# Hyperbolic attention stage: q, k and v kept unscaled beside their factors, with the multiplication moved to each head's preparation

## The reference, cut to what matters

```
q, k, v = heads(x @ Wq.T), heads(x @ Wk.T), heads(x @ Wv.T)       # x is layer-normalized
exp0(u) = tanh(sqrt(c)*|u|) * u / (sqrt(c)*|u|)                   # for q, k, v
dist = arccosh(max(1 + 2c*|q-k|^2 / ((1-c|q|^2)(1-c|k|^2)), 1+1e-5)) / sqrt(c)
weights = softmax(-beta*dist)                                     # 2048 x 2048 for each of 32 heads
out = weights @ log0(v)                                           # then exp0, log0, @ Wo.T, + x
```

## Time and profile before

| | us |
|---|---|
| median of 3 runs | 5894.83 (5894.81 to 5903.06) |
| the profiled execution | 5902.13 |
| its span in the profile | 5900.3 |
| ScalarE busy in the span | 4513.9 (77%) |
| VectorE busy | 4660.2 (79%) |
| TensorE matmul busy | 4364.9 (74%) |
| GpSimd busy | 1432.0 (24%) |

### The profile page before, as it was taken

How to read it: one execution, slowest core, us unless ns; L and a number is a source line. 1 busy time by engine, 2 the same in 40 slices (tenths; PEclk the granted TensorE clock), 3 DMA queues, 4 the chain that set the end, 5 groups by cost and what they waited for, 6 DMA issues and landing times. The chain is left out here.

```text
span 5900.3 us, 69208 instructions
## 1 busy us (share of the span) xinstructions
PE 4364.9 (74%) x22020; PEld 1837.5 (31%) x22020; DVE 4660.2 (79%) x7142; ACT 4513.9 (77%) x3668; POOL 1432.0 (24%) x1259
## 2 busy tenths in 40 slices
PE   8999999999999999546655665665565655655657
PEld 4555555555555556311111011111010111110105
DVE  7666666766666666589989899999998999998966
ACT  4555555555555554339999999999999999999993
POOL 0000000000000000234444444444444444444420
PEclk9999999999999998766666666666666667666667
DMA  1000000000000000169898989898989898989891
GB/s 39 5 5 5 5 7 7 5 5 6 5 5 5 5 2 1 34 171 192 182 193 182 193 182 193 182 193 182 193 182 194 182 193 182 194 182 194 180 197 62
DMA packets 149381, 637.99 MB, mean 108 GB/s; under 512 B 32662, under 2 KB 74840, under 8 KB 79064
## 3 DMA queue, kind: packets, MB, share of 16 engines
q0 software_dynamic: 73728, 536.90, 45.5%
q1 hardware_dynamic: 75224, 95.82, 4.8%
HBM read 69.46 MB, written 26.35 MB: 16 GB/s over the span
## 5 line engine op out<-in xcount | busy, mean ns | idle before, releaser
L1715 PE MATMUL psum<-b_qT,b_kT 126*128 126x512 bf16 x2048 | 921.8, 552 | 1116.0 <-DVE b_tiles L1445 1109.8
L1445 DVE SCALAR_TENSOR_TENSOR b_tiles<-b_ra_rep,b_cap,psum 128x1024 f32<-128x1024 f32 x1024 | 1263.0, 1274 | 281.9 <-DMA b_tiles<-b_tiles 182.1
L668 DVE CUSTOM_DVE_ANT_0 a_srow<-psum,a_bias 128x512 f32<-128x512 f32 (+3 forms) x1280 | 725.6, 607 | 494.2 <-PE psum L849 491.1
L727 ACT ACTIVATE a_pT<-psum 128x512 f32<-128x512 f32 (+3 forms) x1056 | 511.9, 527 | 657.2 <-PE psum L861 656.9
L1715 PEld LDWEIGHTS psum<-b_qT,b_kT 126*128 126x128 bf16 x2048 | 136.4, 108 | 2054.2 <-DVE b_tiles L1445 1882.7
L1452 DVE TENSOR_SCALAR b_tiles<-b_tiles 128x2048 f32<-128x2048 f32 x512 | 682.5, 1333 | 4.3
L861 PE MATMUL psum<-ident,a_srow 128*128 128x128 f32 x4352 | 625.6, 280 | 70.5 <-DVE a_pT L541 32.9
L1728 PE MATMUL psum<-b_tiles,b_v_aug 128*32 128x512 f32 x2736 | 592.0, 957 | 99.7 <-ACT b_tiles L1626 99.7
L1626 ACT ACTIVATE b_tiles<-b_tiles,b_sc 128x4096 f32<-128x4096 f32 x171 | 650.1, 3802 | 5.7
L1618 ACT ACTIVATE b_tiles<-b_tiles 128x4096 f32<-128x4096 f32 x171 | 613.3, 3610 | 35.4 <-DVE b_tiles L1088 34.5
L1295 POOL DMA_DIRECT2D b_tiles<-b_tiles x342 | 355.0, 1229 | 1172.9 <-ACT b_tiles L1618 1169.9
(11 more groups left out here) (215 smaller groups left out, 5338.8 us busy)
## 6 DMA issues: line engine op xcount, KB each, us to landing
b_tiles<-b_tiles POOLq DMA_DIRECT2D x342, 1024.0 KB, 12.9
X<-b_tiles POOLq DMA_DIRECT2D x170, 1024.0 KB, 13.2
b_ra_rep<-ra_scratch SPq DMA_DIRECT2D x32, 1024.0 KB, 13.8
row_scratch<-b_tiles SPq DMA_DIRECT2D x6, 2048.0 KB, 13.9
b_qk_raw<-row_scratch SPq DMA_DIRECT2D x31, 288.0 KB, 8.8
X<-in_x_dram SPq DMA_DIRECT2D x8, 512.0 KB, 6.6
a_wqk<-in_wqk_dram SPq DMA_DIRECT2D x32, 128.0 KB, 2.6
x_scratch<-X SPq DMA_DIRECT2D x4, 1024.0 KB, 10.6
```

The source lines that it names most:

```text
L668: nc.vector.tensor_tensor_reduce(out=srow[:, n % ROWS, h, a:z], in0=bank(c % 2 * 2 + h, 0, z - a), in1=bias[:, h, off + a:off + z], scale= ...
L1445: nc.vector.scalar_tensor_tensor(out=a[:, s * HALF:(s + 1) * HALF], in0=ra_rep[:, j, s * HALF:(s + 1) * HALF], scalar=cap[:, j, k:k + 1], ...
L1715: last = nc.tensor.matmul(half_ps(s)[:, i * BANK:(i + 1) * BANK], kT[:, j, k * P:(k + 1) * P], qT[:, j, cs], start=True, stop=True)
```

## The change: what it does

- `scale` is gone. `tok[b]` is stored to `row_scratch` as projected, and three rows more are stored beside it (F_Q, F_K, F_V: `arr` has seven rows for four). GpSimd's `prepare` and `take_v` multiply by the factor where they copied. Batch 0's q, k, v are stored as soon as its 16 tiles are copied, batch 1's (v first) as soon as all are, each ahead of the factors in SyncE's order.
- `factors` is in three parts. For batch 0, `lengths` is at n = 23 and the parts at n = 24, 26 and 28, each behind the normalization; ScalarE's roots are ahead of the tiles of group 5, the tanh behind them, and the transposes of `ra` one group later.
- Root batches: four of two chunks, then 126 of four; the weights that follow a batch's roots go up to the batch's first chunk.
- GpSimd squares every chunk with c % 4 == 2 from the first on; `first_use` waits are finer and stand with the engine that writes the slot.
- X is saved to its scratch only when the projection's weights are loaded.

```diff
-ROOTS, KEPT = 4, 4
+ROOTS = [2] * 4 + [4] * ((CHUNKS - 8) // 4)
...
-            return SQUARES[c % len(SQUARES)] if c >= NO_POOL else "D"
+            return SQUARES[c % len(SQUARES)]
...
-                step(engine.tensor_copy(aug[:, 0, :, 0:DB], rows(0)))
+                step(engine.tensor_tensor(aug[:, 0, :, 0:DB], rows(0), each(F_Q), ALU.mult))
...
-                step(engine.tensor_copy(aug[:, 1, :, 0:DB], rows(1)))
+                step(engine.tensor_tensor(aug[:, 1, :, 0:DB], rows(1), each(F_K), ALU.mult))
...
-            engine.tensor_copy(v_aug[:, g % 2, :, 0:DB], v).then_inc(S["v_ready"], 1)
+            engine.tensor_tensor(v_aug[:, g % 2, :, 0:DB], v, f.unsqueeze(2).to_broadcast([P, TB, DB]), ALU.mult
+                                 ).then_inc(S["v_ready"], 1)
...
+        def first_use(eng, slot):
+            if slot < 6:
+                eng.wait_ge(S["row_saved0"], 64)
+                eng.wait_ge(S["v_ready"], 1)
+            elif 6 <= slot < 10:
+                eng.wait_ge(S["row_saved1"], 48)
+            elif slot < 12:
+                eng.wait_ge(S["v_saved1"], 16)
...
+            sp.wait_ge(S["w_loaded"], 16)
...
+            sp.wait_ge(S["tok_copied"], TB)
+            for i in range(3):
+                store_row(0, i, S["row_saved0"])
+            store_factors(0)
+            sp.wait_ge(S["ra_stored"], 16)
+            load_ra(0)
+            sp.wait_ge(S["row_saved0"], 64)
+            load_qk(1)
+            load_v(1)
+            load_ra(1)
+            sp.wait_ge(S["tok_copied"], NT)
+            store_row(1, 2, S["v_saved1"])
+            for i in range(2):
+                store_row(1, i, S["row_saved1"])
+            store_factors(1)
...
-            def scale(b):
-                pool.wait_ge(S["factors_done"], b + 1)
-                pool.wait_ge(S["tok_copied"], (b + 1) * TB)
-                for i in SCALED[b]:
-                    dst = tok[b][:, i, :, :, :].rearrange("p h t d -> p (h t) d")
-                    f = tmp[:, FACTOR_OF[i], :].unsqueeze(2).to_broadcast([P, NF, DB])
-                    nc.gpsimd.tensor_tensor(dst, dst, f, ALU.mult).then_inc(S["tok_scaled"], 1)
-
-            scale(0)
-            pool.wait_ge(S["tok_scaled"], 3)
+            pool.wait_ge(S["factors_done"], 1)
+            pool.wait_ge(S["tok_copied"], TB)
...
-            scale(1)
...
+                if c < Y_BACK and by(c) == "P":
+                    first_use(pool, Y_SLOTS[c])
...
-                if n == TB + 4:
-                    factors(0)
+                if n == TB + 7:
+                    lengths(0)
+                if n >= TB + 8 and n % 2 == 0 and n < TB + 14:
+                    factors(0, (n - TB - 8) // 2)
...
-                if n == TB + 3:
-                    lengths(0)
...
+                if q == TB // 4 + 1:
+                    roots_all(0)
...
-                if q == TB // 4:
-                    roots_all(0)
+                if q == TB // 4 + 1:
                     tanhs(0)
-                if q == TB // 4 + 2:
+                if q == TB // 4 + 3:
                     ra_copy(0)
...
-                upto = z - KEPT if z < CHUNKS else CHUNKS
+                upto = a if z < CHUNKS else CHUNKS
```

More of the change, by code:

```diff
@@ L998, in stage_attn_b @@
         sc = sb("sc", [P, 24])
-        NS_Q, E_K, EN_K, CAP_K = range(4)
+        NS_Q, E_K, EN_K, CAP_K, F_Q, F_K, F_V = range(7)
         NF = TB * HB
@@ L1088, in square_by @@
             engine.tensor_tensor(y_slot(c), a, a, ALU.mult).then_inc(S["sq_" + name], 1)
-        root_batches = [(c, min(c + ROOTS, CHUNKS)) for c in range(0, CHUNKS, ROOTS)]
+        root_batches = [(sum(ROOTS[:n]), sum(ROOTS[:n + 1])) for n in range(len(ROOTS))]
+        assert root_batches[-1][1] == CHUNKS
         PREP = 17
@@ L1107, in of, with each @@
                 return f.unsqueeze(2)
+            def each(i):
+                return of(i).to_broadcast([P, TB, DB])
             def rows(i):
@@ L1212, in store_o, with store_row, store_factors @@
                 sp.dma_start(o_scratch[:, g * ROW_K:(g + 1) * ROW_K], o_raw[:, :]).then_inc(S["o_stored"], 16)
-            for b in range(BATCH):
+            def store_row(b, i, saved):
+                hs = slice(b * HB, (b + 1) * HB)
+                at = (0, ROW_K, ROW - ROW_K)[i]
+                sp.dma_start(rows[:, hs, at:at + ROW_K], tok[b][:, i, :, :, :].rearrange("p h t d -> p h (t d)")
+                             ).then_inc(saved, 16)
+            def store_factors(b):
                 hs = slice(b * HB, (b + 1) * HB)
@@ L1219, in _ @@
                 sp.wait_ge(S["factors_done"], b + 1)
[L1220 to L1234, removed]
+                sp.dma_start(rows[:, hs, ROW_F:ROW - ROW_K], arr[b].rearrange("p i h t -> p h i t")
+                             ).then_inc(S[f"row_saved{b}"], 16)
+            sp.wait_ge(S["tok_copied"], TB)
[13 more added lines that the diff above has]
+            store_factors(1)
+            sp.wait_ge(S["row_saved1"], 48)
+            sp.wait_ge(S["v_saved1"], 16)
             sp.wait_ge(S["ra_stored"], 32)
@@ L1388, in lengths, with factors @@
                 nc.vector.tensor_scalar(tmp[:, 2, :], tmp[:, 2, :], col(SC), 1e-30, ALU.mult, ALU.max).then_inc(S["x_all"], 1)
[L1390 removed]
+            def factors(b, part):
                 ar, ns = arr[b], nsq[b]
[L1392 to L1397, removed]
[L1398 to L1413 removed]
@@ new lines, in factors @@
+                if part == 0:
+                    dve.wait_ge(S["th_all"], b + 1)
+                    link(nc.vector.reciprocal(x2, x2))
+                    link(nc.vector.tensor_tensor(f2, f2, x2, ALU.mult))
+                    link(nc.vector.tensor_tensor(n2, f2, f2, ALU.mult))
+                    link(nc.vector.tensor_tensor(n2, n2, ns[:, 0:2, :], ALU.mult))
+                elif part == 1:
+                    nc.vector.tensor_copy(ar[:, NS_Q, :, :], by_head(n2[:, 0, :]))
+                    nc.vector.tensor_copy(ar[:, F_Q, :, :], by_head(f2[:, 0, :]))
+                    link(nc.vector.tensor_scalar(x2, n2, col(NEG_C), 1.0, ALU.mult, ALU.add))
+                    link(nc.vector.tensor_scalar(x2, x2, FLOOR, None, ALU.max))
+                    if b:
+                        dve.wait_ge(S["raT_done"], b)
+                    nc.vector.reciprocal(ra, x2[:, 0, :]).then_inc(S["ra_done"], 1)
+                    nc.vector.tensor_scalar(ar[:, CAP_K, :, :], by_head(x2[:, 1, :]), 1.0 / GUARD, None, ALU.mult)
+                    link(nc.vector.reciprocal(tmp[:, 7, :], x2[:, 1, :]))
+                else:
+                    link(nc.vector.tensor_scalar(tmp[:, 7, :], tmp[:, 7, :], col(C2), None, ALU.mult))
+                    nc.vector.tensor_copy(ar[:, E_K, :, :], by_head(tmp[:, 7, :]))
+                    nc.vector.tensor_tensor(ar[:, EN_K, :, :], by_head(n2[:, 1, :]), by_head(tmp[:, 7, :]), ALU.mult)
+                    link(nc.vector.tensor_tensor(f2[:, 1, :], f2[:, 1, :], tmp[:, 7, :], ALU.mult))
+                    nc.vector.tensor_scalar(ar[:, F_K, :, :], by_head(f2[:, 1, :]), -2.0, None, ALU.mult)
+                    link(nc.vector.reciprocal(tmp[:, 2, :], tmp[:, 2, :]))
+                    link(nc.vector.tensor_scalar(ar[:, F_V, :, :], by_head(tmp[:, 2, :]), col(XMAX), 1.0, ALU.mult, ALU.min))
+                    dve.sem_inc(S["factors_done"], 1)
@@ L1433, in _ @@
             lengths(BATCH - 1)
-            factors(BATCH - 1)
+            for part in range(3):
+                factors(BATCH - 1, part)
             for i in range(4):
@@ L1497, in _ @@
                     if c < A_BACK:
-                        first_use(A_SLOTS[c])
+                        first_use(dve, A_SLOTS[c])
                     argument(g, k)
-                    if 0 < c <= Y_BACK:
-                        first_use(Y_SLOTS[c - 1])
+                    if 0 < c <= Y_BACK and by(c - 1) == "D":
+                        first_use(dve, Y_SLOTS[c - 1])
                     if c:
```

64 lines of the change are left out of this document (20 added, 44 removed).

## The result

The changed kernel takes 5853.66 us (median of 4 runs, 5850.57 to 5859.82), the kernel before 5898.29 beside it (4 runs, 5894.81 to 5903.06): a ratio of 0.9923, 95% interval 0.991 to 0.9935. That is 44.6 us less where 49.4 were forecast; the time is 8.3 above the forecast, 3.5 of which is the median of before, which stood at 5894.83 when the forecast was made. The two profiled executions took 5902.13 (span 5900.3) and 5859.82 (span 5858.0).

The account below looks back on a forecast made before the run. ScalarE bounds the 512-chunk loop, so the gain is how much earlier its full stretch starts: 19.7 us before the first argument plus 29.7 after, 49.4 in all, steady loop zero. Forecast 5845.4 us, range 5828 to 5867.

Parts of the forecast that it names:

- Until T0: Projection up to the loop's first argument (T0): reached 19.7 us earlier, between 16 and 23.
- the 38 that the forecast gave for hidden parts: Projection: first argument 38 us earlier if, against the forecast's reading, the parts of the factors were hidden.
- The start of the loop: From the loop's first argument to the logarithm of chunk 8: 97.8 us against 127.5, so 29.7 less.
- 15.4 + 69.7 + 12.7 of waits = 97.8: Loop start, in us: first root at 15.4, then ScalarE's work and its waits until the logarithm of chunk 8.
- rival 1: Loop start gains less because GpSimd's early squares make more waits or hold VectorE up: 5858 us, chance 0.2.
- the wait ahead of root 14: Loop start: ScalarE waits 4.5 us because chunk 15's argument, with seven A buffers, needs the sum of chunk 8.
- the landmark: Logarithm of chunk 8 in the loop, at 2685.80 us before the change; forecast 98 us after the first argument (2636).
- the 69.7: Loop start: ScalarE's work in us, 8 root pairs x 3.57, 4 weight pairs x 7.4, 9 table loads x 1.29.
- the 2.66: Us per ScalarE table switch by the Trainium skill, drain included; the forecast set it aside for the rows' 1.29.
- Steady loop: GpSimd's three copies per head become multiplications, up to 1.3 us a head more, under its idle time: cost zero.
- Rival 3: Slower: GpSimd's multiplications delay the sums in the steady loop, 133 us lost, 5978 us; chance 0.04.
- Rivals 2 and 4: Factors hidden, 9 to 16 us more gained, 5833 (0.1); first argument not earlier because of SyncE's queue, 5885 (0.03).

Follow-up runs that it names:

- e5: Changed kernel with batch 0's lengths and factors whole in one stop at the old place, n = 20: 5861.40 us, 0.9932 of the kernel before.
- e4: Changed kernel with batch 0's factor parts behind the fourth normalization of a group (n = 27, 31, 35), transposes of `ra` one group later: 5845.25 us.
- e3: Changed kernel with GpSimd's squares of chunks 2 and 6 issued ahead of the sums of the batch before them: 5851.28 us.
- e6: Changed kernel with the first twelve squares all on VectorE, as before the change: 5858.43 us.
- e1: Changed kernel with only the moved multiplication, earlier stores, loads and finer waits kept; batches of four, early squares on VectorE, factors whole: 5857.47 us.
- e2: Changed kernel with root batches of four chunks from the start, nothing else: 5855.44 us.
- e7: Changed kernel with root batches of two chunks throughout, 252 more table loads: 6214.26 us, 1.0531 of the kernel before.

## Why the prediction was right, and where it was off

**Until T0: right, term by term.** 19.95 us measured from the start of the stage, 19.7 forecast. Parts 0 and 1 with the tanh cost 12.3 (12.0 forecast). The second group lost 4.7, part 2 with what GpSimd adds, for which 3.9 and 1.0 were taken; three normalizations beside GpSimd's preparation took 1.48 in place of about 1.04. TensorE's matmuls behind the two stops took 11.73 for a group and 22.14 for the last two, against 10.48 and 20.80, where one group had lost 1.55 before: 1.0 added, 1.5 forecast. e5 confirms the reading that this work is in series, and e4 the reason: VectorE gives the normalizations behind it. Put behind the fourth normalization, the parts leave T0 at 148.91, 39.0 before that of the kernel before: which is the 38 that the forecast gave for hidden parts, and takes another place for the parts and not their division. SyncE's queue did no harm: in VectorE's waits between T0 and 2640 there is none for a DMA.

**The start of the loop: the step that was mis-sized is "15.4 + 69.7 + 12.7 of waits = 97.8".** The first root begins at T0 + 15.8 (15.4 forecast; the 19 in the list of signs is its end, at 19.4). The waits are 17.7: 8.11 ahead of root 2 (7.4 forecast), 4.41 ahead of root 10 (none forecast), 5.18 ahead of root 14 (4.5), none ahead of the first weights (0.8). The rest, 0.8, lies in the gaps between instructions. So it is 104.0, and 23.4 us gained where 29.7 were forecast. This is the second half of rival 1 (VectorE held up by GpSimd's squares), at 6.3 us of its 12.7: VectorE loses 8.5 in its squares. e3 takes away the order that causes it and gives 98.5. That this is within 0.7 of the forecast is in part luck: its waits are 5.7, 1.9, 0 and 4.6, where the sum had 7.4, 0.8, 0 and 4.5.

**A right number with a wrong reason.** I put the wait ahead of root 14 to seven A buffers and the sum of chunk 8. VectorE's list of waits has no such entry. Square 15 ends at 2638.32, 99.0 behind T0, after VectorE had worked without a pause. The row that I leaned on, a wait of 1.75 for a sum in the earlier trace rows, belongs to the steady loop. I laid out ScalarE's time in detail and never VectorE's up to the same point. Without hold-ups VectorE's instructions until the end of square 15 come to 88.2 us (99.0 less 8.8 lost in squares and 2.0 in clamps), and the layout has ScalarE free for root 14 at 97.8 - 3.57 - 1.29 - 4.5 = 88.4. The two engines are level there, so everything above a few tenths that holds VectorE up shows at the landmark. The same omission hid what small batches do. They let ScalarE reach its first weights sooner, worth 2.0 to 2.7 us (e6 against e1, e3 against e2), and in the changed kernel they also put GpSimd's squares behind the sums and beside VectorE's, which costs more than that: 2.9 us on balance (e2).

**Table switches.** 1.29 for each was in the 69.7; e7 has 1.40 to 1.43 as the cost of one switch more, with the pair of roots taking 7.12 at once in the earlier trace rows where two single ones take 3.64 each. The rows were the better guide than the 2.66.

**Steady loop: zero, right.** GpSimd's lines by shape over 2700 to 5600, after the change:

```profile
L1134 POOL TENSOR_TENSOR b_aug<-b_qk_raw 128x256 f32<-128x256 f32 x29 | 44.8, 1544 | 0.0
L1170 POOL TENSOR_TENSOR b_v_aug<-b_v_raw 128x256 f32<-128x256 f32 x30 | 26.6, 887 | 0.0
...
L1139 POOL TENSOR_TENSOR b_aug<-b_qk_raw 128x256 f32<-128x256 f32 x29 | 17.9, 618 | 0.0
```

The multiplication of k (L1139) takes 618 ns where the copy took 399. The 0.40 that the forecast took for all three copies holds for k alone: over the same stretch q's took 1309 ns in the mean before and takes 1544 now, v's 575 and 887. That is 0.8 us a head more, of 1.3 at most forecast, and it stays under GpSimd's idle time: 3082.76 against 3082.64 for the loop. Rival 3 is refuted. Batches are still 24.5: a load at 2658.16 and the pair of roots from 2659.46, 7.13 long.

**Rivals 2 and 4.** The factors were not hidden, and T0 did move.

**The total.** 43.4 us until the landmark against 49.4, 43.3 until the last square; the spans differ by 42.3, the medians by 44.6. What lies outside the stage varies by up to 11 us ahead of it and 6 behind it from one kernel's profile to the next, so medians can't confirm a term of a few us (e5's lies 7.7 above the changed kernel's with the same stage); the landmarks can.

Open: why the head and the tail vary. And e4 and e3 were tried at one place each; whether part 2 of the factors or the second factors can be hidden further was not.

## What to carry to other kernels

For each stretch, lay out the work of every engine up to the same landmark before you explain the waits of one: an engine that isn't the bound of the kernel as a whole can set the end of the stretch. That it is busy all the time doesn't yet show it (in e2 VectorE is, and ScalarE sets the end); what shows it is which of the two waited for the other last. Where two engines hold each other up, their order in the queues decides, here at least: put GpSimd's instruction where VectorE's next ones are of the kind that isn't held, ahead of DMA issues rather than behind them. And work that an engine does between its turns in a pipeline is hidden only behind all that the others wait for; cutting it in pieces ahead of that hides nothing.

## What the runs showed of the hardware

- A VectorE square of 128x2048 in float32, 2.28 us alone, took 5.92 and 6.70 when a GpSimd square of the same size ran beside it: it ends some 2.2 us after GpSimd's, so it waits for all that is left of it. In e3 the half arguments, which read PSUM (1.24 each), kept their pace beside GpSimd's square, and only the clamp behind them was held, 2.50 for 1.2. The Trainium skill (SBUF — State Buffer, SBUF: two separate sides) has an exclusive lock that whichever of the two engines starts first keeps for its whole instruction, for an operation of VectorE with two SBUF inputs or in a two-port mode. The trace agrees for the first of the two squares, 3.64 us lost of 3.76 left; for the second, VectorE's record starts 0.28 ahead of GpSimd's and it is still VectorE that is held, so the part on who starts first isn't shown here.
- A table switch costs 1.40 to 1.43 us in all (e7), of which the load itself is 1.28.
- A GpSimd multiplication of 128x256 in float32 by a broadcast factor took 0.62 for q, k and v of head 0, where the copies took 0.40. In the loop, means are 1.54, 0.62 and 0.89 for q, k and v, where the copies had 1.31, 0.40 and 0.58. Single ones of q and v take either some 0.6 or 1.6 there, right behind a GpSimd square; no run settles which it is and why.
- The time ahead of the stage varied over 11 us and the tail over nearly 6 between executions of nearly the same program, while the 3082 us from the logarithm of chunk 8 to the last square repeated within 0.5.
